# Attention block: row normalisation moved behind the mix, and the sixth group of query blocks transposed through transfers

## The reference

```python
y = ((xg - mu) * rsqrt(var + EPS)).reshape(B, C, H, W)      # 4 groups of channels
y = y * gn_gamma[None, :, None, None] + gn_beta[None, :, None, None]
qkv = einsum('bchw,dc->bdhw', y, w_qkv) + b_qkv
scores = einsum('bnc,bcm->bnm', q, k) * C ** (-0.5)
w = softmax(scores, axis=-1)
a = einsum('bnm,bmc->bnc', w, v)
out = einsum('bchw,dc->bdhw', a, w_out) + b_out
return x + out
```

## Time and profile before

| what | us |
|---|---|
| median of 3 timed runs | 146.07 |
| lowest and highest of them | 144.9, 148.31 |
| span of the profiled execution, first to last instruction | 143.7 |
| TensorE busy in that span | 133.6 |
| VectorE busy | 103.9 |
| ScalarE busy | 67.7 |
| POOL busy | 57.1 |

### The profile page before, as it was taken

One profiled execution on the slowest core, in us unless ns is written; L12 is line 12 of the kernel. 1 busy time (PEld: TensorE's weight loads), 2 busy tenths in 40 slices (PEclk: granted clock), 3 DMA queues, 4 the chain that ended last, 5 costly groups with the idle time before them and its releaser, 6 DMA issues.

```text
span 143.7 us, 1862 instructions
## 1 busy us (share of the span) xinstructions
PE 133.6 (93%) x589; PEld 94.4 (66%) x589; DVE 103.9 (72%) x201; ACT 67.7 (47%) x122; POOL 57.1 (40%) x66
## 2 busy tenths in 40 slices
PE   7999999997499979997999999999999999999990
PEld 7978579873367635665655556766776666768770
DVE  0597587799978999899496987898763787463402
ACT  3164858763266526543361364455843666353000
POOL 6032347963334666633355556433543213330000
PEclk9999999999999999999999999999999999999998
DMA  4940000000045976983598539973996001000211
GB/s 159 310 188 0 0 5 0 0 2 0 0 101 117 206 165 141 206 200 109 109 203 197 152 66 206 206 182 81 212 203 168 0 0 73 0 0 0 80 70 73
DMA packets 6154, 15.07 MB, mean 105 GB/s; under 512 B 1664, under 2 KB 1664, under 8 KB 6144
## 3 DMA queue, kind: packets, MB, share of 16 engines
q1 hardware_dynamic: 5856, 14.69, 41.3%
q10 hardware_dynamic: 288, 0.27, 0.5%
HBM read 2.36 MB, written 2.10 MB: 31 GB/s over the span
## 4 chain that ended last, share of the span: by engine, by line
PE 66%; DVE 14%; SPq 7%; issue 5%; ACT 4%; DMA 2%; DVEq 0%
PE mixed L765 22%; SPq L235 7%; PE scores L715 5%; PE scores L714 5%; PE turned L731 5%; PE scores L717 5%; DVE scores L527 5%; PE scores L773 4%; DVE crossed L552 4%; ACT probs L366 3%; PE mixed L760 3%; PE mixed L762 3%; PE mixed L761 3%; PE turned L661 2%; PE mixed L661 2%
## 5 line engine op out<-in xcount | busy, mean ns | idle before, releaser
L295 POOL TENSOR_SCALAR probs<-probs,inv_sum 128x1024 f32<-128x1024 f32 x32 | 35.9, 1122 | 63.7 <-DVE inv_sum L532 63.7
L527 DVE TENSOR_SCALAR_CACHE_REDUCE scores<-scores,key_bias 128x1024 f32<-128x1024 f32 x31 | 40.0, 1289 | 13.9 <-PE scores L717 13.8
L366 ACT ACTIVATE probs<-scores,neg_max 128x1024 f32<-128x1024 f32 x32 | 35.7, 1115 | 18.7 <-DVE scores L527 17.7
L765 PE MATMUL mixed<-crossed,v 128*128 128x512 f32 x80 | 37.7, 593 | 1.0 <-DMA crossed<-crossed 1.0
L714 PE MATMUL scores<-y_hi,z_hi 128*128 128x512 f32 x62 | 34.6, 558 | 0.3 <-DVE z_lo L489 0.3
L552 DVE STREAM_TRANSPOSE crossed<-probs 128x1024 f32<-128x1024 f32 x20 | 24.8, 1241 | 0.0
L715 PE MATMUL scores<-y_lo,z_hi 128*128 128x512 f32 x62 | 24.4, 394 | 0.0
L765 PEld LDWEIGHTS mixed<-crossed,v 128*128 128x128 f32 x80 | 14.1, 190 | 11.6 <-issue 11.0
L717 PE MATMUL scores<-y_hi,z_lo 128*128 128x512 f32 x62 | 19.3, 392 | 0.0
L714 PEld LDWEIGHTS scores<-y_hi,z_hi 128*128 128x128 f32 x62 | 11.7, 189 | 8.8 <-issue 5.7
L715 PEld LDWEIGHTS scores<-y_lo,z_hi 128*128 128x128 f32 x62 | 11.7, 189 | 7.0 <-issue 5.5
(11 more groups left out here) (147 smaller groups left out, 168.9 us busy)
## 6 DMA issues: line engine op xcount, KB each, us to landing
crossed<-crossed SPq DMA_DIRECT2D x80, 128.0 KB, 2.3
out_dram<-result SPq DMA_DIRECT2D x8, 256.0 KB, 2.5
xs<-in_x_dram SPq DMA_DIRECT2D x2, 512.0 KB, 6.4
xs<-in_x_dram SPq DMA_DIRECT2D x3, 256.0 KB, 5.0
xs<-in_x_dram ACTq DMA_DIRECT2D x1, 256.0 KB, 3.5
ws<-in_weights_dram SPq DMA_DIRECT2D x1, 256.0 KB, 3.7
vecs<-in_vectors_dram ACTq DMA_DIRECT2D x1, 3.0 KB, 3.9
```

Of the source, the lines that this page charges most:

```text
L295: pool.tensor_scalar(probs[:, i % RING, :], probs[:, i % RING, :], inv_sum[:, i:i + 1], 1.0, ALU.mult, ALU.mult).then_inc(s_probs, 1)
L366: act.activation(probs[:, i % RING, :], scores[:, i % 2, :], ACT.Exp, bias=neg_max[:, i:i + 1], scale=-1.0, accum_out=row_sum[:, i:i + 1]) ...
L527: dve.tensor_scalar(scores[:, i % 2, :], scores[:, i % 2, :], key_bias[:, b % 2, i:i + 1], None, ALU.subtract, ALU.min, accum_out=neg_max[ ...
L765: mm = pe.matmul(bank, v[:, b % 2, k, :], at, start=first, stop=final)
```

## The change

1. The blocks of groups 0 to 6 are no longer normalised. `flip` and, for group 0, `turn` take the exponentials as they are. VectorE makes the inverse sums of a group's four blocks in one instruction (`group_inverse_sums`). SyncE writes these 128 x 4 values to a scratch in DRAM (`inv_out`, ahead of the group's swap) and reads them back as one row spread to all 128 partitions (`inv_in`, behind the swap). When a group is mixed, VectorE multiplies the bank by that row (`scaled`), and POOL adds the input (`residual`), to which ScalarE has added the output bias before (`add_out_bias`, at i = 5).
2. Group 6 goes the way of groups 1 to 5: flips and a swap, no transposes on TensorE. When its swap has landed, ScalarE copies heads (`swapped_heads`, four pairs of key tiles, at steps 30 and 31, around the copies of blocks 30 and 31) and VectorE leaves the tails in place (`last_tails`). It is mixed whole after the loop.
3. Group 7 keeps its normalisation and its transposes. It is mixed in two halves of 256 queries, one before and one behind group 6 (`mix_last`), and has its results and stores in halves.
4. The statistics come two steps earlier (i = 2 and 3), the product with `minus_mean` is replaced by a subtraction on VectorE (`negated_means`), and the tail of z is made on POOL for both halves, from a copy by ScalarE.

The core of the diff:

```diff
-    SWAPPED = range(1, 6)
-    SPLIT_GROUPS = (6, 7)
+    SWAPPED = range(1, 7)
+    LAST = GROUPS_OF_FOUR - 1
+    PARTED = {group: () for group in range(1, 6)} | {6: (0, 1, 2, 3)}
...
-           27: [(5, 2)], 28: [(5, 3)], 29: [(5, 2)], 30: [(5, 1), (6, 3)], 31: [(6, 5)]}
+           27: [(5, 2)], 28: [(5, 2)], 29: [(5, 2)], 30: [(5, 2)]}
...
+            def inv_out(group):
+                sp.wait_ge(s_inv, group + 1)
+                sp.dma_start(inv_scratch[group, :].rearrange("(u p) -> p u", u=QB),
+                             inv_sum[:, QB * group:QB * group + QB],
+                             allow_slow_non_contiguous=True).then_inc(s_scratch, 16)
+            def inv_in(group):
+                sp.wait_ge(s_scratch, 16 * (group + 1))
+                if group >= 2:
+                    sp.wait_ge(s_scaled, group - 1)
+                sp.dma_start(inv_rows[:, group % 2, :],
+                             inv_scratch[group:group + 1, :].to_broadcast([128, HALF])).then_inc(s_inv_rows[group % 2], 16)
...
-            swap(1)
-            for group in range(2, 6):
-                swap(group)
-                store(group - 2)
-            for group in range(4, GROUPS_OF_FOUR):
-                store(group)
+            inv_out(0)
+            inv_in(0)
+            for group in SWAPPED:
+                inv_out(group)
+                swap(group)
+                inv_in(group)
+                if group >= 2:
+                    store(group - 2)
+            store(5)
+            store(6)
...
+            def residual(group):
+                pool.wait_ge(s_scaled, group + 1)
+                pool.tensor_tensor(result[:, g, :], result[:, g, :], xs[:, b, g * HALF:(g + 1) * HALF],
+                                   ALU.add).then_inc(s_result, 1)
...
+            def swapped_heads(group, pair):
+                act.wait_ge(s_swapped[group % 2], swaps(group))
...
+                act.activation(head_pair(group, pair), home_pair(group, pair).bitcast(fp32),
+                               ACT.Copy).then_inc(s_head, 1)
...
+                    if n >= 30:
+                        swapped_heads(6, 2 * (n - 30))
+                    if not swapped(n):
+                        turned_copy(n)
+                    if n >= 30:
+                        swapped_heads(6, 2 * (n - 30) + 1)
...
             def flip(n):
-                dve.wait_ge(s_probs, n + 1)
+                dve.wait_ge(s_exp, n + 1)
...
+            def scaled(group):
+                dve.wait_ge(s_mixed, KT * (group + 1))
+                dve.wait_ge(s_inv_rows[g], 16 * (group // 2 + 1))
...
+                dve.tensor_tensor(result[:, g, :], mixed[:, g, :], inv_rows[:, g, :], ALU.mult).then_inc(s_scaled, 1)
...
-                    if b + 2 < BATCHES and i in (4, 5):
-                        half_stats(b + 2, i - 4)
+                    if b + 2 < BATCHES and i in (2, 3):
+                        half_stats(b + 2, i - 2)
...
+            last_tails(0)
+            turned_tails(30)
+            scaled(5)
+            last_tails(1)
+            turned_tails(31)
+            last_tails(2)
+            last_tails(3)
+            last_result(0, mixed[:, 1, 0:256])
+            scaled(6)
+            last_result(1, scores[:, 0, 0:256])
...
-            mix(GROUPS_OF_FOUR - 1, KT)
+            mix_last(0, mixed[:, 1, 0:256])
+            mix(6, KT)
+            mix_last(1, scores[:, 0, 0:256])
```

More of the change, by code:

```diff
@@ L121, in attention_kernel @@
-        PT_HI, PT_LO = {6: pt_hi_6, 7: pt_hi_7}, {6: pt_lo_6, 7: pt_lo_7}
+        staging_even = sb("staging_even", [128, GROUP])
+        with nc.sbuf_tensor("last_turned_head", [128, KT, HALF], fp32r) as pt_hi:
+            pass
+        staging_odd = sb("staging_odd", [128, GROUP])
+        STAGING = (staging_even, staging_odd)
+        with nc.sbuf_tensor("first_turned", [128, KT, HALF], fp32) as first_turned:
+            pass
+        home_even = sb("home_even", [128, GROUP], fp32r)
+        home_odd = sb("home_odd", [128, GROUP], fp32r)
@@ L122, in attention_kernel @@
+        HOME = (home_even, home_odd)
+        heads = sb("heads", [128, PAIRS, N], fp32r)
+        inv_rows = sb("inv_rows", [128, 2, HALF])
         result = sb("result", [C, 2, HALF])
+        inv_scratch = nc.dram_tensor("inv_scratch", [GROUPS_OF_FOUR, HALF], fp32).ap()
         scores = ps("scores", [128, 2, N])
@@ L617, in _ @@
                         maximum(*ahead)
[L618 to L621 removed]
+                    if n < QB:
+                        turned_copy(n)
+                    if QB * LAST <= n < 30:
+                        turned_tails(n)
+                    if swapped(n + 1):
+                        flip(n + 1)
+                    if i % QB == 2 and n // QB < LAST:
+                        group_inverse_sums(n // QB)
                     if i == 0 and b > 0:
@@ L735, in _, with three_products @@
             tiles_mixed = [0] * GROUPS_OF_FOUR
+            def three_products(bank, value, head, tail, first, final):
+                value_hi, value_lo = value
+                pe.matmul(bank, value_hi, head, start=first, stop=False)
+                pe.matmul(bank, value_hi, tail, start=False, stop=False)
+                return pe.matmul(bank, value_lo, head, start=False, stop=final)
             def mix(group, count):
@@ L758, in mix @@
[L758 to L767 removed]
+                    first, final = k == 0, k == KT - 1
```

376 lines of the change are left out of this document (218 added, 158 removed).

## The result

The changed kernel takes 152.79 us (median of 4 runs, 150.61 to 154.26) beside 146.01 for the kernel before: ratio 1.0379, 95% interval 1.0292 to 1.0466. The forecast was 144.6 with a range of 141.2 to 148.6: the wrong side and outside the range. Two later sets gave 148.43 and 147.62, the latter with ratio 1.0128 (1.0044 to 1.0211): slower there too, but by less than the 2% that count as clear. Why the sets differ so much belongs to the finding. The ratios leave disturbed executions out.

The account below looks back on a forecast made before the run. TensorE, busy 93% of the span, was taken as the bound. Stages -2.1 - 3.8 + 3.3 - 0.5 gave -3.1 us; +1.6 for the clock made -1.5, from 146.07 to 144.6 us, range 141.2 to 148.6.

Parts of the forecast that it names:

- Rival 2: SyncE's queue: each microsecond of scatter over 0.6 delays groups 1 and 6 in full; up to 148.2 us, chance 0.2.
- Stage A: Run up to the start of group 1's mix: flip of block 7 earlier, scatter added, mix at 51.75, -2.1 us.
- hold an engine at most 1.3 us: Before group 1's mix: bound on the scatter's 512 small packets, at 0.04 us each at most on 16 engines.
- the 3.6 us worked out by it: Scatter at one descriptor per element: its price would be 1.84 us and the sum about 3.6 us dearer.
- Stage B: Group 1's mix to the end of group 4's last tiles: fewer transposes, no statistics wait, -3.8 us.
- slack of 0.7: Swaps for groups 3 and 5: TensorE needs about 15 us until the mix, the transfer 14.2.
- Stage C: Group 4's last tiles to TensorE's last matmul: new wait for group 6's swap before block 31's transposes, +3.3 us.
- Stage D: Last addition and store after TensorE's last matmul: half the columns and half the bytes, -0.5 us.
- The clock: TensorE's gaps before group 1's mix and block 31's transposes: one clock fall of the two likeliest, +1.6 us.
- the 3.2 worked out there: Clock cost if both TensorE gaps lower it, by the skill's rule: +3.2 us, leaving no change in time.
- Rival 3: Group 6's mix: strided tiles stream slower, 24 matmuls at twice the price cost 5.6 us, 150.2 us; chance 0.05.

Follow-up runs that it names:

- rows of 16 bytes: Changed kernel with the scatter writing 128 pieces of 16 bytes for 512 of 4, groups 0 to 6 normalised by wrong sums: 142.01 us, ratio 0.9644.
- sums in rows: Changed kernel with the scratch written in 128 pieces of 16 bytes and VectorE's scaling reading that order, whole reference computed: 143.44 us, ratio 0.9865.

## Why the prediction was wrong

The chance of the wrong side was on record as Rival 2, "the scatter holds SyncE's queue (slower)", with 0.2. It had the right culprit and the wrong resource: it priced the scatter's issue, with ends 0 and 1.84 us, and the issue was 0.37. The step that failed is Stage A's sentence that 512 small packets "hold an engine at most 1.3 us". Of the engines that was true: the scatter's packets took 0.25 us on each of 16. (The bound was wide: the 288 packets of the earlier trace rows from which it was worked out carry 0.9 KB each on average.) But SyncE could go on only when the writes had landed, and that was 8.95 us. No bound was set on the landing of the scatter, nor on the landings and the issues of what follows it: the sum took 2.29 us for the one and 10.1 for the other as they were before. The Trainium skill's rule that the prediction cited there (DMA: Bandwidth & Descriptors, Rules for kernel authors), one descriptor per element, pointed at the scatter too; the 3.6 us worked out by it were also too few.

Stage by stage on the profiled spans:

- **Stage A**, -2.1 forecast, +0.2 measured (mix of group 1 at 54.08 against 53.85). SyncE started swap 1 at 37.90; by the forecast it is 40.24 - 2.1 = 38.1. VectorE's 2.8 us were right (the flip of block 7 ended at 37.40 instead of 40.21), and from there to swap 1 it took 0.5 for the forecast 0.7. SyncE's long issue cost 0.9 less than before (1.32 for 2.22). The landing, 5.74 for 2.29, is the miss. In the second profile of the same kernel group 1's mix began at 54.06 by the other way, with 14.69 us of issues and a landing of 2.33.
- **Stage B**, -3.8 forecast. From the mix of group 1 to the end of group 4's last tiles (111.15 + 1.72 = 112.87) it took 58.8 us against 59.95, so -1.2. Of the missing 2.6 us, 2.1 are the three tiles at the lower clock (4.92 for 2.81); the clock stood in a term of its own. Another 0.25 is TensorE's wait for swap 3, whose last transfer landed after 5.87 us; the prediction had given group 3 a slack of 0.7. The wait for the statistics went, as forecast.
- **Stage C**, +3.3 forecast: 36.8 us (112.87 to 149.66) for 26.63, so +10.2, with 2.6 of the clock in it. The place was right, TensorE idle ahead of block 31's transposes behind swap 6; the size was 7.98, of which 5.3 are SyncE's 15.36 us for 10.03. The other profiles agree: with 13.47 us of issues the gap was 6.10, twice, and with 10.04 (rows of 16 bytes) 2.61. The 256-column matmuls were 0.12 us, under the 0.135 taken.
- **Stage D**, -0.5 forecast, -0.4 measured (2.84 for 3.27).
- **The clock**, +1.6 for one fall of two. Both gaps let it fall: it cost 2.1 us behind the first, and behind the second the transposes and group 7's first half took 6.3 us (134.66 to 140.96) where 0.87 and 24 times 0.12 make 3.7, so 2.6. The rule of the Trainium skill that the prediction cited (TensorE: Matmul & The Clock Gate, Why this matters for your kernels), by which both gaps cost, agrees with this trace: 4.7 for the 3.2 worked out there.

With the landing mended the rest can be read: with sums in rows the mix of group 1 began at 50.22 (forecast 51.75), the gap ahead of block 31 was 3.80 (forecast 3.3), the clock fell once, at that gap, and the time was 143.4 against 144.6. So the plan of the other steps held, and one unpriced landing, with what it held up and what that did to the clock, made the difference. Rival 3 did not show: group 6's strided products came 0.24 us apart, as 512 columns do in rows 5. Not tried: the statistics and the tails of z each by themselves.

## What to carry to other kernels

Price a transfer by three numbers, its issue, its packets and its landing, and ask for each what is queued behind it; a few KB can hold up 128 KB. When a wait ends in a transfer, look also at the issues ahead of its last one: here 5.3 us ahead of block 31 stood there and not in a landing. Write small vectors to memory in pieces as wide as the layout allows, and let the reader undo the order: here 16 bytes a row and a strided read on VectorE took 143.4 where the four-byte scatter took 147.6 to 152.8. And where an engine does two independent chains at the end, put the one that doesn't wait for a transfer first; that alone was worth some 4 us or more here.

## What the runs showed of the hardware that was not expected

- Packed four-byte writes to DRAM landed after 7.0 to 9.0 us, though their packets took 4.0 us of 16 engines' time together; the same 512 writes 64 bytes apart landed within 2.1 us.
- Transfers between SBUF and SBUF that touch no DRAM waited behind them: the last one of swap 1 landed in 5.74 us instead of 2.29 on the same queue, and in 7.61 with the writes on another.
- Gaps of 1.17, 1.51, 2.32 and 3.03 us ahead of group 1's mix left the granted clock as it was in their profiles; behind gaps of 2.11, 2.46 and 2.73 it fell. Length alone did not tell in these profiles.
- SyncE's queue lost up to 5.91 us in a single issue. All 57 of its issues of 0.95 us or more, in 19 profiles, coincide with a packet of the instruction queues, and such packets took up to 5.4 us beside packed four-byte writes and up to 2.7 without them. No run was made to separate the two.
